# Linear attention and mixture of experts in one Trainium2 kernel: LayerNorm rows turned by a transposing DMA, k rows likewise, a new order within a step, own spare rows

## The chip, the cores and the metric

The kernel runs on one NeuronCore of a Trainium2 chip. The number that counts is the device time of one execution in microseconds (us); lower is better. TensorE is called PE below (its weight loads PEld), VectorE DVE, ScalarE ACT, GpSimd POOL and SyncE SP. SP computes nothing here: it issues DMAs, in order.

## The reference, cut to what matters

Shapes: x is 4 x 2048 x 256 in fp32. Attention has 16 heads of 16 features and is causal and linear; the feed-forward part has 8 experts with 512 hidden features, and each token goes to its best two.

```python
x = x + attn(layernorm(x))
    # q, k = elu(xWq + bq) + 1, elu(xWk + bk) + 1 ; v = xWv + bv
    # per token: s += k v^T ; z += k ; value = q s / (q z + 1e-6) ; out = value Wo + bo
x = x + moe(layernorm(x))
    # logits = x router^T ; top 2, softmax over them
    # out = sum over the two experts e of p_e * (gelu(x w1[e]^T + b1[e]) w2[e]^T + b2[e])
```

## The kernel before, in words

The kernel has two parts.

**Attention part** (about the first 640 us). The sequence is cut into 16 steps of 128 positions; a step holds the 4 batches, so 4 x 128 tokens. The work is software-pipelined over steps. In body c, the *front* handles step c (LayerNorm rows turned, q, k, v projections, feature map), the *back* handles step c-1 (scores within the chunk, attention, running state), `ro` finishes step c-2 (output projection, residual, second LayerNorm, router), and `sc` gives slots to the rows of step c-3 and scatters them to the experts' rows in DRAM. The first bodies are written out: body 0, then body 1 with the front alone, then body 1 with the back alone, then 2 to 4. Bodies 5 to 14 are a hardware loop with two bodies per round, and the rest is written out again.

The order on each engine is the order in which `body` writes it, one function per engine; semaphores join them. Nothing is rescheduled.

Values that need more than fp16 are split in two fp16 parts, high and low, and multiplied in three passes (`split3`). The names that matter:
- `xs`: x of one step as loaded; `xn`: its LayerNorm, with tokens on partitions (ACT, `normalise`, L748). PE turns `xn` (`x_transposes`, L442) into the banks pF, ACT takes the high part (`x_hi`, L787) and DVE the low part (`x_lo`, L1029) into `xT`, with features on partitions. `project(0..3)` (L422) reads `xT`.
- `feature(m)` (POOL, L1385) ends the feature map of q (m = 0, 1) and k (m = 2, 3); `qk_high` and `low` (L811, L1389) split it into `qkhl`. SP stores q, waits for the landing, loads the stack `qst` in 6 DMAs, then does the same for k with 3 DMAs into `kst` (L347, L363, L358). The scores (L494, L497) read both stacks.
- k with tokens on partitions: PE turns the fp32 `kf` (`k_rows`, L480) and ACT copies it to `kn` (L773). The state update reads `kn` and `v` in fp32 (L527).
- Scores: ACT takes the high part (`score_hi`, L781) and DVE the low part (`score_lo`, L1024), 16 of each a step. The second LayerNorm is applied on DVE (`norm2_apply`, L1037); the router's gap and second probability are two small DVE operations (L1108, L1125).

**Expert part** (from about 670 us). 71 tiles of 256 rows run in a loop. Each tile is loaded, turned, sent through two layers, and its rows are added to the output by indirect DMAs from POOL (L1485). Rows that fill up a tile, and whole tiles that fill up the 71, add zeros to one shared block of 256 spare output rows. POOL waits before a tile until as many earlier additions have landed as `settled` says (L1306): for a tile of an expert, those of all tiles ahead of that expert's first; for a tile behind the last expert, those of all tiles ahead of itself.

Of the kernel before, what the change touches and what calls it, by code (L numbers as in the profile page):

```python
# [50 lines left out]
C_POW, C_LN, C_PAD, C_TOKEN, C_END = 280, 284, 285, 287, 287 + STEPS * B  # L51
# [4 lines left out]
def constants():  # L56
# [11 lines left out]
    f[:, C_PAD:C_PAD + 2] = T + p[:, None] + P * np.arange(2)  # L68
# [11 lines left out]
def build(nc, x, wqkvo, bqk, bv, bo, rw, w1, b1, w2, b2, cf, ch, cb, out):  # L80
# [5 lines left out]
    with ExitStack() as ctx:  # L86
# [18 lines left out]
        pads = sb("pads", [P, 2, ROW], F32)  # L105

# [6 lines left out]
        v = sb("v", [P, 2, B, H, VC], F32, att)  # L113
# [21 lines left out]
        xn = sb("xn", [P, B, D], F32, att)  # L135
        xT = sb("xT", [P, 2, KC, B * C], F16, att)
        et = sb("et", [P, 2, B * C], F32, att)
        lt = sb("lt", [P, 2, B * C], F32, att)
        kn = sb("kn", [P, B, D], F32, att)
# [27 lines left out]
        spare = xn[:].rearrange("p b d -> p (b d)")  # L167
# [34 lines left out]
        route_copy = lambda c, b: xn[:, b] if c == STEPS + 1 else xn2T[:, b % 2].rearrange("p k n -> p (k n)")  # L202
# [7 lines left out]
        passed = {nc.vector.engine: sem("passed_dve"), nc.gpsimd.engine: sem("passed_pool")}  # L210
# [8 lines left out]
        pads_set, pads_out = sem("pads_set"), sem("pads_out")  # L219
# [5 lines left out]
        xT_ps, xT_hi, xT_lo = sem("xT_ps"), sem("xT_hi"), sem("xT_lo")  # L225
# [4 lines left out]
        kn_ps, kn_done = sem("kn_ps"), sem("kn_done")  # L230
# [12 lines left out]
        TAB = 19  # L243
# [69 lines left out]
        def _(sp):  # L313
# [9 lines left out]

            def body(j, c, front=True, back=True):
                i, _ = front_of(j, c)
                r, _ = front_of(j, c - 2)
                fr, ro, nx = front and real(j, c), real(j, c - 2), front and real(j, c + 1)
                for n in range(0 if c == 1 else 2 if c == 0 else 1 if nx else 0):

                    sp.wait_ge(xn_done, 4 * (i + n) + 4)  # L330
                    sp.dma_start(xs[:], x_steps[bass.ds(i + n + 1, 1)].rearrange("i p b d -> p (i b) d")).then_inc(x_in, 16)
# [3 lines left out]
                if fr:  # L335
# [5 lines left out]
                    for t, sent in enumerate((q_out, k_out)):  # L341
                        sp.wait_ge(qk_hi, 4 * i + 2 * t + 2)
                        sp.wait_ge(qk_lo, 4 * i + 2 * t + 2)
                        if c >= 2 and t == 0:

                            sp.wait_ge(stack_in[par], 144 * (j + c // 2))
                        sp.dma_start(qk_dram[par, t].rearrange("m p n -> p m n"), qkhl[:, t]).then_inc(sent, 16)  # L347
                        sp.wait_ge(sent, 16 * i + 16)
                        if t == 0 and c >= 2:
# [65 lines left out]
        def _(pe):  # L415
            def split3(out, lhs, rhs, n, parts=((0, 0), (0, 1), (1, 0)), low_wait=None):

                terms = [(a, b_, k) for a, b_ in parts for k in range(n)]
                for t, (a, b_, k) in enumerate(terms):
                    if low_wait and t == 2 * n:  # L420
                        pe.wait_ge(*low_wait)
# [3 lines left out]
            def body(j, c, front=True, back=True):  # L425
# [157 lines left out]
                if bk:  # L583
                    scores(0, 0)
# [941 lines left out]
```

## Time and profile before

| | |
|---|---|
| median of 3 runs | 1098.19 us (1097.6 to 1102.02) |
| profiled execution | 1098.38 us, span 1096.6 us |
| mean granted TensorE clock | 0.957 |
| busy: PE, DVE, ACT, POOL | 953.8, 823.6, 662.1, 695.6 us |
| DMA | 138.18 MB, mean 126 GB/s |

Busy time counts each engine's own instructions. In the profile an idle time is put down to what ended it, and a DVE or POOL instruction that has started but is held still counts as busy. The attention part and the expert part have different limits, so the shares of the whole span say little about either.

### The profile page before, as it was taken

Reading aid. Unit: us, or ns where it says so; the run is one execution under the profiler, and the core shown is the slowest. Engines: PE = TensorE matmul, PEld = TensorE weight load, DVE = VectorE, ACT = ScalarE, POOL = GpSimd, SP = SyncE. Lnnn points to the kernel's source line nnn. Section 1 sums busy time; section 2 is a strip of 40 time slices with the busy share of each in tenths; the row PEclk is TensorE's granted clock in tenths of the full one; section 3 lists DMA queues with packets and bytes.
Section 4 is the critical chain, followed back from the end, with each engine's and each line's share of the span. In section 5 each row is a group of like instructions: output and inputs, shape, how many; then the busy total and the mean of one; then the engine's idle time right before and its main releaser. Section 6 shows DMA issues by size and latency. Waiting matters only on the chain. (4 is left out here: it accounts for less than half of the span.)

```text
span 1096.6 us, 33544 instructions
## 1 busy us (share of the span) xinstructions
PE 953.8 (87%) x10092; PEld 786.4 (72%) x10093; DVE 823.6 (75%) x2201; ACT 662.1 (60%) x1253; POOL 695.6 (63%) x606
## 2 busy tenths in 40 slices
PE   4499888988897998889998935999999999999993
PEld 2277667766775775766677724999999999999992
DVE  5378999997997997988998874666666666666662
ACT  5567776776676676766775433555555555555550
POOL 5626576787677777775878452555665565665554
PEclk9989999999999998999999966999999999999997
DMA  3665766556654673664466282455555555555553
GB/s 110 151 139 129 201 166 155 130 154 170 151 124 134 161 162 112 169 159 111 148 143 163 72 320 77 87 96 96 89 91 94 92 96 96 87 92 95 92 87 38
DMA packets 124885, 138.18 MB, mean 126 GB/s; under 512 B 10320, under 2 KB 117968, under 8 KB 124176
## 3 DMA queue, kind: packets, MB, share of 16 engines
q1 hardware_dynamic: 96944, 100.26, 37.3%
q0 software_dynamic: 26688, 35.93, 17.7%
q10 hardware_dynamic: 1184, 1.18, 0.4%
q8 instruction: 29, 0.48, 0.2%
q14 instruction: 40, 0.33, 0.1%
HBM read 72.00 MB, written 65.34 MB: 125 GB/s over the span
## 5 line engine op out<-in xcount | busy, mean ns | idle before, releaser
L1485 POOL DMA_INDIRECT out<-yt,to_token x142 | 226.8, 1597 | 177.4 <-DVE yt L1349 108.7
L1024 DVE SCALAR_TENSOR_TENSOR ahl<-pS,ahl 128x512 f16<-128x512 f32 x240 | 161.4, 682 | 34.8 <-ACT ahl L781 33.1
L781 ACT ACTIVATE ahl<-pS 128x512 f16<-128x512 f32 x240 | 140.8, 599 | 71.1 <-PE pS L497 69.0
L1403 POOL DMA_INDIRECT expert_in<-xn,cur x128 | 130.7, 1021 | 35.2 <-issue 33.1
L422 PE MATMUL pF<-xT,was 128*128 128x512 f16 x384 | 104.6, 415 | 14.5 <-DVE xT L1029 14.4
L949 ACT ACTIVATE g<-pS,b1s 128x256 f32<-128x256 f32 x144 | 60.4, 471 | 90.6 <-PE pS L422 90.6
L494 PE MATMUL pS<-cbs 128*128 128x512 bf16 x240 | 94.4, 393 | 20.0 <-DMA kst<-qk_parts 14.2
L1320 DVE TENSOR_TENSOR ghl<-g,ghl 128x1024 f16<-128x1024 f32 x71 | 87.2, 1228 | 24.4 <-ACT ghl L971 24.4
L422 PE MATMUL pU<-w2s,ghl 128*128 x864 | 100.5, 273 | 1.9 <-DVE ghl L1320 1.9
L422 PE MATMUL pS<-gT,w1s 128*128 128x256 f16 x864 | 101.3, 274 | 0.1
L422 PE MATMUL pF<-w2s,ghl 128*128 x840 | 97.4, 273 | 0.0
L497 PE MATMUL pS<-qst,kst 96*128 96x256 f16 x480 | 94.8, 279 | 0.0
L422 PEld LDWEIGHTS pU<-w2s,ghl 128*128 128x128 f16 x864 | 84.4, 98 | 12.1 <-issue 2.5
L422 PEld LDWEIGHTS pS<-gT,w1s 128*128 x864 | 85.0, 98 | 10.8 <-issue 0.5
L1361 POOL TENSOR_TENSOR rs<-ve,cfs 128x4 f32<-128x4 f32 x32 | 33.0, 1031 | 93.1 <-DVE ve L994 93.1
L518 PE MATMUL pO<-vhl,ahl 128*128 128x17 f16 x3072 | 87.4, 171 | 2.1 <-DVE ahl L1024 2.1
L518 PEld LDWEIGHTS pO<-vhl,ahl 128*128 128x128 f16 x3072 | 85.6, 96 | 4.6 <-DVE ahl L1024 2.7
L422 PEld LDWEIGHTS pF<-w2s,ghl 128*128 128x128 f16 x840 | 82.2, 98 | 9.1
L422 PEld LDWEIGHTS pF<-xT,was 128*128 128x128 f16 x384 | 38.6, 104 | 55.3 <-issue 21.8
L971 ACT ACTIVATE ghl<-g 128x1024 f16<-128x1024 f32 x71 | 75.6, 1065 | 0.1
L497 PEld LDWEIGHTS pS<-qst,kst 96*128 96x128 f16 x480 | 48.5, 101 | 36.8 <-issue 5.2
L949 ACT ACTIVATE g<-pO,b1s 128x256 f32<-128x256 f32 x70 | 29.4, 470 | 71.6 <-PE pO L422 71.6
(160 smaller groups left out, 2308.8 us busy)
## 6 DMA issues: line engine op xcount, KB each, us to landing
xg<-expert_in SPq DMA_DIRECT2D x71, 260.0 KB, 3.0
qk_parts<-qkhl SPq DMA_DIRECT2D x32, 512.0 KB, 2.9
qst<-qk_parts SPq DMA_DIRECT2D x96, 128.0 KB
kst<-qk_parts SPq DMA_DIRECT2D x48, 256.0 KB
xs<-x SPq DMA_DIRECT2D x16, 512.0 KB, 5.1
xr<-x SPq DMA_DIRECT2D x16, 512.0 KB, 4.7
out<-x SPq DMA_DIRECT2D x16, 512.0 KB, 3.2
expert_in<-pads SPq DMA_DIRECT2D x16, 260.0 KB, 4.0
```

Of the source, the lines that this page charges most:

```text
L422: mm = nc.tensor.matmul(out, lhs(a, k), rhs(b_, k), start=(t == 0), stop=(t == len(terms) - 1))
L494: nc.tensor.matmul(o[:], ident16, mask16, start=True, stop=False, skip_group_check=True)
L497: mm = nc.tensor.matmul(o[:, e * 2 * C:(e + 1) * 2 * C], kst[0:STACK, sp_, pr, b * C:(b + 1) * C], qst[0:STACK, sp_, pr, :, b * C:(b + 1) ...
L518: mm = nc.tensor.matmul(pO[:, h * VC:(h + 1) * VC], ahl[:, b % 2, a, h * C:(h + 1) * C], vhl[:, sp_, b_, b, h * VC:(h + 1) * VC], start=False,
L781: nc.scalar.activation(ahl[:, b % 2, 0, n * 4 * C:(n + 1) * 4 * C], score_bank(fr, n)[:], ACT.Relu).then_inc(sc_hi, 1)
L949: nc.scalar.activation(g[:, p1, f], hidden[p1][f // 2][:, (f % 2) * MT:(f % 2 + 1) * MT], ACT.Gelu, bias=b1s[:, bass.ds(e * FC + f, 1)], s ...
L971: nc.scalar.activation(ghl[:, p1, 0].rearrange("p f n -> p (f n)"), g[:, p1].rearrange("p f n -> p (f n)"), ACT.Copy).then_inc(g_hi, 1)
L1024: V.scalar_tensor_tensor(ahl[:, b % 2, 1, cols], score_bank(fr, n)[:], 0.0, ahl[:, b % 2, 0, cols], ALU.max, ALU.subtract).then_inc(sc_lo, 1)
L1320: V.tensor_tensor(ghl[:, p1, 1].rearrange("p f n -> p (f n)"), g[:, p1].rearrange("p f n -> p (f n)"), ghl[:, p1, 0].rearrange("p f n -> p ...
L1361: G.tensor_tensor(rs[:], ve[:], cfs[:, C_POW:C_POW + B], ALU.pow).then_inc(done, 1)
L1403: G.indirect_dma_start(xg_dram, bass.IndirectOffsetOnAxis(ap=cur[:, qp, 2 * b + t:2 * b + t + 1], axis=0), xn2[:, qp, b], None).then_inc(s ...
L1485: G.indirect_dma_start(out, bass.IndirectOffsetOnAxis(ap=to_token[:, c % 2, s:s + 1], axis=0), yt[:, c % 2, s], None, compute_op=ALU.add). ...
```

## The change

1. **x.** ACT normalises `xs` in place and takes the high part of all four batches in one operation (`x_high`); DVE takes the low part in one operation (`x_low`) into `xhl`, still with tokens on partitions. SP issues one transposing DMA per step from `xhl` to `xT`, which is now double-buffered. All of this is done in the body before the one that uses it. PE's `x_transposes`, ACT's `x_hi` and DVE's `x_lo` are gone.
2. **k.** `kn` holds fp16 high and low parts and is filled by a transposing DMA from what SP stored of k in DRAM. PE's `k_rows` and ACT's copies are gone. The state update is three fp16 passes over `kn` and `vhl`, where it was one fp32 product.
3. **Order within a step.** The projections stand earlier on PE, the feature operations earlier on ACT, the statistics of the next step's x earlier on DVE, and both reciprocal roots in POOL stand in the middle.
4. **Spare rows.** The output has a block of 256 spare rows for each of the 8 possible filling tiles besides the shared one; the blocks are zeroed by 8 more DMAs of 256 KB in body 2, and one DMA in body 3 writes 2048 row numbers. `settled` is zero for filling tiles.
5. **VectorE forms.** `norm2_apply` was a TENSOR_SCALAR and two small router operations were TENSOR_TENSOR; all three are now SCALAR_TENSOR_TENSOR.
6. `v` has one buffer instead of two.

```diff
+            sp.wait_ge(x_lo, 1)
+            sp.dma_start_transpose(xT[:, 0]..., xhl[:]...).then_inc(xT_in, 16)
...
-                for n in range(0 if c == 1 else 2 if c == 0 else 1 if nx else 0):
-                    sp.wait_ge(xn_done, 4 * (i + n) + 4)
-                    sp.dma_start(xs[:], x_steps[bass.ds(i + n + 1, 1)]...).then_inc(x_in, 16)
+                if nx:
+                    sp.dma_start(xs[:], x_steps[bass.ds(i + 1, 1)]...).then_inc(x_in, 16)
+                if bk:
+                    if c >= 2:
+                        sp.wait_ge(u_ps, 4 * s)
+                    sp.dma_start_transpose(kn[:], qk_dram[(c - 1) % 2, 1]...).then_inc(kn_in, 16)
...     (q and k stored, stacks loaded, as before)
+                if turn_next:
+                    if c >= 1:
+                        sp.wait_ge(v_ps, 2 * i)
+                    sp.wait_ge(x_lo, i + 2)
+                    sp.dma_start_transpose(xT[:, (c + 1) % 2]..., xhl[:]...).then_inc(xT_in, 16)
...
+                        sp.dma_start(out[T + (n + 1) * MT:T + (n + 2) * MT]..., pads[:, :, 0:D]).then_inc(spare_out, 16)
...
                 def project(m):
                     if m == 0:
-                        pe.wait_ge(xT_lo, 2 * i + 1)
-                        pe.wait_ge(xT_hi, 2 * i + 2)
+                        pe.wait_ge(xT_in, 16 * i + 16)
...
-                    pe.wait_ge(kn_done, 2 * s + 2)
+                    if b == 0:
+                        pe.wait_ge(kn_in, 16 * s + 16)
...
-                        mm = nc.tensor.matmul(pU[...], kn[:, b, k * P:(k + 1) * P], v[:, sp_, b, ...], start=True, stop=True)
+                        mm = split3(pU[...], lambda a, _: kn[:, b, (KC * a + k) * P:...],
+                                    lambda a, _: vhl[:, sp_, a, b, ...], 1)
...
+            def x_high(i, first=False):
+                act.wait_ge(xn_done, 4 * i + 4)
+                if not first:
+                    act.wait_ge(xT_in, 16 * i)
+                nc.scalar.activation(xhl[:, :, 0], xs[:], ACT.Copy).then_inc(x_hi, 1)
...
+            def x_low(i):
+                dve.wait_ge(x_hi, i + 1)
+                V.scalar_tensor_tensor(xhl[:, :, 1], xs[:], 1.0, xhl[:, :, 0], ALU.mult, ALU.subtract).then_inc(x_lo, 1)
...
-                    V.tensor_scalar(xn2[:, rp, b, 0:D], x1[:, b], mv2[:, b, 0:1], rs2[:, b:b + 1], ALU.subtract, ALU.mult)
+                    V.scalar_tensor_tensor(xn2[:, rp, b, 0:D], x1[:, b], mv2[:, b, 0:1],
+                                           rs2[:, b:b + 1].to_broadcast([P, D]), ALU.subtract, ALU.mult)
...
-                    V.tensor_tensor(pd[:, 0], mx[:, :, 1], mx[:, :, 0], ALU.subtract)
+                    V.scalar_tensor_tensor(pd[:, 0], mx[:, :, 1], 1.0, mx[:, :, 0], ALU.mult, ALU.subtract)
...
-            chain(V.scalar_tensor_tensor(tj[0:1, 3], tj[0:1, 0], float(E), tj[0:1, 2], ALU.is_ge, ALU.mult))
-            chain(V.tensor_tensor(first_i[:, 0], tj[0:1, 1], tj[0:1, 3], ALU.add))
+            chain(V.scalar_tensor_tensor(first_i[:, 0], tj[0:1, 0], float(E), tj[0:1, 1], ALU.is_lt, ALU.mult))
```

`turn_next` is true in the bodies that prepare the next step: body 0, the second half of body 1, and every later body that has a next step.

The order on PE at the start of body 2 before (`pF<-cfs,xn` are the turns of x, `pU<-cfs,kf` those of k, `pF<-xT,was` a projection, `pS<-...` the scores, `pO<-...` the attention, `pU<-v,kn` the state update):

```order
L480 MATMUL pU<-cfs,kf 128x128 x4
L422 MATMUL pF<-xT,was 128x512 x6
L494 MATMUL pS<-cbs 128x512
L497 MATMUL pS<-qst,kst 128x256 x2
L422 MATMUL pA<-was,aT 128x256 x6
L422 MATMUL pF<-xT,was 128x512 x6
L494 MATMUL pS<-cbs 128x512
L497 MATMUL pS<-qst,kst 128x256 x2
L480 MATMUL pU<-cfs,kf 128x128 x4
```

The same place now, from the first projection's end on:

```order
L457 MATMUL pF<-xT,was 128x512 x6
L548 MATMUL pA<-cfs,at 128x128 x2
L505 MATMUL pS<-cbs 128x512
L508 MATMUL pS<-qst,kst 128x256 x2
L457 MATMUL pF<-xT,was 128x512 x6
L457 MATMUL pA<-was,aT 128x256 x6
L505 MATMUL pS<-cbs 128x512
L508 MATMUL pS<-qst,kst 128x256 x2
```

The turns of k have left PE, and the third projection stands right behind the third score group.

The order of SP's DMAs in bodies 0 and 1 before, from the load of the k stack of step 0:

```order
L358 DMA kst<-qk_parts 32x8x512 x3
L367 DMA w1raw<-w 128x512
L338 DMA xr<-x 128x4x256
L347 DMA qk_parts<-qkhl 128x4x512
L363 DMA qst<-qk_parts 16x8x512 x6
L347 DMA qk_parts<-qkhl 128x4x512
L358 DMA kst<-qk_parts 32x8x512 x3
```

The same stretch now:

```order
L378 DMA kst<-qk_parts 32x8x512 x3
L391 DMA_TRANSPOSE xT<-xhl 128x16x128
L396 DMA w1raw<-w 128x512
L339 DMA xs<-x 128x4x256
L352 DMA xr<-x 128x4x256
L366 DMA qk_parts<-qkhl 128x4x512
L383 DMA qst<-qk_parts 16x8x512 x6
L366 DMA qk_parts<-qkhl 128x4x512
L378 DMA kst<-qk_parts 32x8x512 x3
L345 DMA_TRANSPOSE kn<-qk_parts 128x4x512
```

The transposing DMA of step 1's x stands behind the first k stack, and that of step 0's k rows stands behind the second, whose data are step 1's.

## Rows read from the trace of the kernel before

**Rows 1.** Windows view, 13 steps, last line: total us, busy sums, then means per step.

```profile
sum 488.00, PE 437.06 PEld 338.80 DVE 436.79 ACT 349.70 POOL 348.16; mean PE 33.62 PEld 26.06 DVE 33.60 ACT 26.90 POOL 26.78
```

**Rows 2.** DVE groups by form, 100 to 560 us: busy, mean ns | idle before.

```profile
L1037 DVE TENSOR_SCALAR xn<-x,mv,rs 128x256 f32<-128x256 f32 x48 | 36.6, 803 | 0.0
L1108 DVE TENSOR_TENSOR pd<-mx 128x4 f32<-128x4 f32 x12 | 22.0, 1837 | 0.0
...
L1125 DVE TENSOR_TENSOR xn<-pd,one_exp 128x4 f32<-128x4 f32 x12 | 16.0, 1330 | 0.0
```

**Rows 3.** Tile xn: count, duration ns min/median/max, first and last start.

```profile
L1037 DVE TENSOR_SCALAR xn<-x,mv,rs x64: 398/410/1469, 91.0 to 639.0; 128x256 f32<-128x256 f32 x64
...
L1125 DVE TENSOR_TENSOR xn<-pd,one_exp x16: 155/1172/2177, 120.1 to 646.4; 128x4 f32<-128x4 f32 x16
```

**Rows 4.** POOL and DVE timelines at 257 us: start, us, operation [idle before <-releaser].

```profile
257.08 2.37 POOL L1365 TENSOR_TENSOR xr<-xr,bos 128x1024 f32<-128x1024 f32 x1
```

```profile
257.66 1.82 DVE L1108 TENSOR_TENSOR pd<-mx 128x4 f32<-128x4 f32 x1
...
263.75 1.29 DVE L1029 TENSOR_TENSOR xT<-pF,xT 128x512 f16<-128x512 f32 x2 [2.47 <-issue]
```

**Rows 5.** POOL and DVE timelines at 96 us.

```profile
96.43 2.72 POOL L1389 TENSOR_TENSOR qkhl<-kf,qkhl 128x512 f16<-128x512 f32 x2
```

```profile
96.49 1.65 DVE L1144 SCALAR_TENSOR_TENSOR w1s<-w1raw,w1s 128x512 f16<-128x512 f32 x1
```

**Rows 6.** PE timeline across the turn of the loop.

```profile
251.95 0.71 PE L527 MATMUL pU<-v,kn 128*128 128x136 f32 x4
...
253.42 1.47 PE L422 MATMUL pF<-was,xT 128*128 128x256 f16 x12
...
257.88 1.04 PE L442 MATMUL pF<-cfs,xn 128*128 128x128 f32 x8
...
261.69 0.60 PE L480 MATMUL pU<-cfs,kf 128*128 128x128 f32 x4
...
264.57 1.68 PE L422 MATMUL pF<-xT,was 128*128 128x512 f16 x5 [2.09 <-DVE xT L1029]
```

**Rows 7.** SP timeline, one step of the loop: issue times.

```profile
279.45 0.37 SPq L347 DMA_DIRECT2D qk_parts<-qkhl  x1
282.48 2.70 SPq L363 DMA_DIRECT2D qst<-qk_parts  x6
285.28 0.38 SPq L347 DMA_DIRECT2D qk_parts<-qkhl  x1
291.71 1.35 SPq L358 DMA_DIRECT2D kst<-qk_parts  x3
```

**Rows 8.** PE, POOL and SP timelines, bodies 0 and 1.

```profile
36.12 4.45 PE L422 MATMUL pF<-xT,was 128*128 128x512 f16 x12 [3.06 <-DVE xT L1029]
...
60.80 0.71 PE L527 MATMUL pU<-v,kn 128*128 128x136 f32 x4
```

```profile
46.56 1.16 POOL L1389 TENSOR_TENSOR qkhl<-qf,qkhl 128x512 f16<-128x512 f32 x1
```

```profile
48.48 1.29 SPq L358 DMA_DIRECT2D kst<-qk_parts  x3
...
60.67 0.38 SPq L347 DMA_DIRECT2D qk_parts<-qkhl  x1
67.20 1.30 SPq L358 DMA_DIRECT2D kst<-qk_parts  x3
```

**Rows 9.** Page, DMA issues: KB each, median us to landing.

```profile
expert_in<-pads SPq DMA_DIRECT2D x16, 260.0 KB, 4.0
```

**Rows 10.** POOL and DVE timelines, the last tiles.

```profile
1074.49 2.49 POOL L1485 DMA_INDIRECT out<-yt,to_token  x1 [2.65 <-DMA out<-yt,to_token]
...
1081.82 1.55 POOL L1485 DMA_INDIRECT out<-yt,to_token  x1 [2.79 <-DMA out<-yt,to_token]
...
1088.26 1.55 POOL L1485 DMA_INDIRECT out<-yt,to_token  x1 [2.83 <-DMA out<-yt,to_token]
```

```profile
1081.21 0.69 DVE L1344 SCALAR_TENSOR_TENSOR yt<-pU,b2s 128x512 f32<-128x512 f32 x1 [4.38 <-DMA out<-yt,to_token]
```

More of the change, by code:

```diff
@@ L373, in body @@
                                      pads[:]).then_inc(pads_out, 16)
+                        sp.dma_start(out[T + (n + 1) * MT:T + (n + 2) * MT].rearrange("(s p) d -> p s d", p=P),
+                                     pads[:, :, 0:D]).then_inc(spare_out, 16)
+                if c == 3:
+                    sp.wait_ge(pads_out, 16 * E)
+                    with nc.allow_non_contiguous_dma("one number per row"):
+                        sp.dma_start(xg_dram[DUMMY:ROWS, TOKEN:TOKEN + 1].rearrange("(s p) d -> p (s d)", p=P),
+                                     dummy_token[:]).then_inc(pads_out, 16)
                 if c == STEPS:
@@ L856, in body @@
                     w2_high(1)
+                if bk:
+                    score_hi(0, 2)
                 if fr and c >= 2:
@@ L907, in body @@
                     row_copy(3)
+                if turn_next:
+                    x_high(i + 1)
                 if bk:
                     score_hi(2, 3)
-                if bk:
                     score_hi(3, 0)
                     score_hi(3, 1)
-                left = c == 1 and not front
-                if nx and c != 1 or left:
-                    normalise(i + 1, 0)
-                if bk:
                     score_hi(3, 2)
@@ L920, in body @@
                     out_hi(s, 2)
-                if nx and c != 1 or left:
-                    normalise(i + 1, 1)
-                if fr and c != 1 or left:
+                if fr and c != 1 or c == 1 and not front:
                     v_high()
@@ L1018, in body @@
                 nx = front and real(j, c + 1)
+                turn_next = nx and c != 1 or c == 1 and not front
                 par, sp_, rp, qp = c % 2, (c - 1) % 2, c % 2, (c - 3) % 2
@@ L1414, in body @@
                     feature(0)
+                    feature(1)
+                    low(0)
                 if ro:
                     rstd(r, ve2, rs2, ln2_ve, ln2_rs)
+                if nx and c >= 2 or c == 1 and not front:
+                    rstd(i + 1, ve1, rs1, ln1_ve, ln1_rs)
                 if fr:
-                    feature(1)
-                    low(0)
                     feature(2)
```

250 lines of the change are left out of this document (110 added, 140 removed).

## The prediction

> **What bounds the kernel now.** I read the page's busy shares first, then a table of windows over the attention part, then DVE's groups, then timelines of single engines around each place that the change touches. The reader is to see two things. In the attention part PE and DVE are both nearly full: over 13 steps of 37.54 us (488.0 / 13) PE is busy 33.62 us and DVE 33.60 us a step [rows 1], so each is idle for 3.9 us. In the expert part PE alone is full and nothing there is changed but its last tiles. So the steps are won only as far as DVE gets shorter or idles less; relieving PE alone is not enough.
>
> Part of DVE's busy time is no work. The four-element operation L1125 takes 0.155 us at best and 1.33 us on average, L1037 0.40 at best and 0.80 on average [rows 2, 3]. L1108, of the same size as L1125, averages 1.84 us. One instance shows why: it starts at 257.66 and ends at 259.48, and the POOL operation that started at 257.08 ends at 259.45 [rows 4]. DVE is held until POOL is done. Per step that is 1.68 (L1108) + 1.18 (L1125) + 4 x 0.40 (L1037) = 4.5 us.
>
> **The change, part by part.** The sum is made against the profiled execution, 1098.38 us, 0.2 us above the median of the three runs.
>
> *PE's work.* The turns of x (1.04 us) and of k (2 x 0.60) go [rows 6]. A state update was 0.71 us for a pair in fp32. It becomes 6 fp16 matmuls of 136 columns; the row of 256 columns gives 0.12 us each (1.47 / 12), so at most 0.7 and by width 0.4 us: 4 x 0.3 = 1.2 saved, at least nothing. PE loses 2.2 to 3.4 us of work a step. On a DVE-bound step this counts only through DVE's idle time.
>
> *DVE's work.* Both `x_lo` go, 1.29 us [rows 4]. `x_low` has 1024 elements, as many as the two together, so 1.2 us. The statistics, moments and shift of the next step's x only move. Net: -0.1 us a step.
>
> *The VectorE forms.* Between none and all of the 4.5 us could go. The rows say none: L1144 already is a SCALAR_TENSOR_TENSOR with two SBUF inputs, and it took 1.65 us while a POOL operation begun 0.06 us ahead of it ran [rows 5], as a TENSOR_TENSOR does. All three new forms read two SBUF tensors. I take 0 for the form itself. What the new order does to these meetings I can't work out; POOL's work per step stays the same, and `x_low` is one more operation with two SBUF inputs, that can meet POOL's 2.37 us operation [rows 4]. I take 0, bounds 2.4 lost and 2.5 gained a step.
>
> By the Trainium skill (SBUF — State Buffer, "SBUF: two separate sides") the port pair that DVE shares with GpSimd is an exclusive lock, taken by a DVE operation in a two-port mode or with two SBUF inputs, the latter only against a GpSimd operation that reads SBUF. By that rule the new forms are held as the old ones were, which the trace's 1.65 us bears out; if the form decided, the steps would gain up to 4.5 us more.
>
> *DVE's idle time.* Of 3.9 us a step, at the turn of the loop 2.47 us stand ahead of `x_lo`, put down to "issue", every second step [rows 4], and PE waits 2.09 us for its result [rows 6]. Now PE has a score group and the first two projections to run without DVE there, since `xT` came a step earlier, so the restart behind the gap is quick, though DVE's own gap stays. The other idle is DVE waiting for scores, which PE reaches sooner by 2 to 3 us of freed work. I take 3.9 down to 2.1, so 1.8 gained a step; bounds 0 and 3.
>
> *ACT.* It loses two copies for x and two for k, and gains `x_high`. It was 26.90 us busy of 37.5 [rows 1]; hidden either way.
>
> *SP's queue in the loop.* Before, q's store was issued at 279.45, its stack at 282.48, k's store at 285.28, k's stack at 291.71 [rows 7]. k's store alone took 6.4 us, since it stood behind the q stack. By the new order on PE, where the third projection stands behind the third score group, I estimate the projections 8 us and, since POOL's features follow only in part, k's store 4 us earlier, which pays for the transposing DMA of x behind the k stack. That must land before the next step's first projection. By these rows I place its issue 8 us after k's store, and its landing 4 to 7 us later (512 KB; the like store took 3.0 us alone and 6.4 us in the queue). That is just at the start of the next step. I take no wait; the other end is a rival. The k rows' DMA is issued at the start of the body and needed behind four score groups and three projections, which I estimate at 12 us in.
>
> *The start.* This is the largest single term, and it is a loss. SP works in order, and the transposing DMA of step 1's x stands behind step 0's k stack. That was issued from 48.48 to 49.77 [rows 8]; I leave it there, within 3 us. With 4 to 5 us for landing, `project(0)` of step 1 starts at 54 where it started at 36.12. From that projection to the end of q's low parts it took 11.6 us (36.12 to 47.72), so q's store goes at 65.6, its landing takes 3, its stack 2.8 to issue, and k's store and stack follow 6.5 us apart (60.67 to 67.20): k's stack of step 1 at 78. The k rows of step 0 are asked for behind it, at 79, and land at 84. PE's first state update began at 60.80 and waits for them. That is 23 us. Even if nothing of step 1 came later, it would be 67.20 + 1.3 + 4.5 = 73, 12 us late; at slow transposes 28. PE is in order, and everything behind it in body 1 waits. I take +23.
>
> *Spare rows.* 8 more DMAs of 256 KB in body 2, and 2048 single numbers in body 3. DMAs of 260 KB land in 4.0 us each [rows 9]; 8 more at the rate of this size hold the rings some 7 us, in which the k rows of step 2 wait. There are about 12 us of slack. I take +2, bounds 0 and 6.
>
> *The last tiles.* POOL's idle time in front of three filling tiles' first additions, 2.65 + 2.79 + 2.83 us [rows 10], is a wait for the landing of the tile ahead. With own rows it goes. Next is DVE: it waited 4.38 us for the landing two tiles back (1081.21), which now comes earlier too. Not all is won, as POOL's additions then stand back to back behind the tile ahead: -6.5, bounds -5.5 and -8.3.
>
> Sum: 1098.4 + 23 + 2 - 6.5 - 14 x 1.8 (25.2; the 13 steps of the table and the next) = 1091.7, say **1092**.
>
> **The rivals.**
>
> *B. POOL's holds become rare.* The reorder or the new forms avoid most of the 4.5 us. For it: this is the only large time on DVE that is no work. Against it: L1144's row. Then 4.0 a step: 1098.4 + 18.5 - 56 = 1061.
>
> *C. The steps gain almost nothing (slower).* DVE stays as full as it is, because `x_low` is held behind POOL and PE's freed time turns into waits for DVE. For it: 33.60 busy of 37.54, and only 0.1 us of DVE's work goes. It decides when the gain per step is below 18.5 / 14 = 1.3 us, since the start must be paid for. With 0.5 a step: 1098.4 + 18.5 - 7 = 1110.
>
> *D. The transposing DMA lands late in every step.* PE's first projection then waits for it, and all behind it. The place has no slack by my reckoning, so each us beyond 7 costs 1 us a step. At 11 us from issue to landing a step gets 1.8 - 4 = 2.2 us longer and the start 31 us: 1098.4 + 31 - 4.5 + 31 = 1156. The trace of before has no such DMA; 512 KB in 3.0 us speaks against it, the 6.4 us in the queue for it. The Trainium skill gives both sides: VectorE: DVE Perf Modes, "The three transpose paths", has 1309 ns for one 128x128 block, so 21 us as an estimate for 16 blocks one after another; DMA: Bandwidth & Descriptors, "Latency and other measured facts", has 261 GB/s, an estimate of 2 us. No run here shows either yet.
>
> *E. The start costs less.* If body 1's front is not delayed, it is +12 instead of +23: 1081.
>
> **How the numbers follow.** Half a per cent is 5.5 us, about what a measurement of this kernel can tell from no change. Chances: forecast 0.34 (own range 1080 to 1104), B 0.18, C 0.28, D 0.12, E 0.08. Faster by over 0.5%: half of the forecast, B and E, 0.43. Within 0.5%: a third of the forecast and a quarter of C, 0.19. Slower: the rest of the forecast, of C, and D, 0.38. The range, 1064 to 1128, leaves out the far half of B and most of D.
>
> **What would show it.** Start: PE's first `pU` matmul waits for `kn` until 80 to 88. Steps: a mean of 35 to 36.5 us, DVE busy 33 to 34, with the new L1099 (the gap) and L1116 still far above 0.16 us when POOL computes; under B they fall to it. Under D the first projection of each step waits for DMA `xT`. Tail: POOL's last additions no longer wait for a landing, and 5.5 to 8 us go. The forecast is wrong if PE doesn't wait at the start, or if a step comes out under 34.5 or over 37 us.

## The result and the profile after

The changed kernel takes 1203.47 us (median of 4 runs, 1202.7 to 1208.27), the kernel before 1097.89 us beside it (1095.53 to 1102.02). The ratio is 1.098, 95% interval 1.0945 to 1.1017. I had forecast 1092, with a range up to 1128. Ratios leave out disturbed runs; so for two kernels below (`fixed` and `thin_old`) the ratio is lower than the median alone would give.

| | before | after |
|---|---|---|
| span of the profiled execution | 1096.6 us | 1206.5 us |
| mean granted TensorE clock | 0.957 | 0.904 |
| busy: PE, DVE, ACT, POOL | 953.8, 823.6, 662.1, 695.6 | 964.2, 824.2, 636.3, 698.1 us |
| step 4, DVE's first reciprocal of the attention | 200.1 us | 250.7 us |
| step 14, the same | 577.4 us | 687.0 us |

No engine got more work to speak of. The time is idle time, 110 us of it ahead of 690 us: 51 in the first five bodies, 59 in the ten steps of the loop. The last steps lose 6 more (the first addition of the expert part is issued at 802.8 us, before at 687.1), and the last tiles win 6 back. The last row of the windows view, 12 steps from 166.7 us on, answers to [rows 1]: total, busy sums, means per step.

```profile
sum 520.30, PE 408.97 PEld 294.87 DVE 405.47 ACT 300.74 POOL 335.62; mean PE 34.08 PEld 24.57 DVE 33.79 ACT 25.06 POOL 27.97
```

A step takes 43.36 us (520.3 / 12) where it took 37.54. PE and DVE are busy about as before; each is idle for 9.3 us and more where it was 3.9. So neither bounds the step: they wait for each other. PE's own figure hides a change: the turns of x and k are gone and the state update is shorter, 2.7 us less a step together, but the rest of its matmuls, the same in number, took 3.2 us more. The granted clock was 0.86 to 0.96 in these steps, where it was 0.92 to 1.00.

DVE's groups by form, 100 to 700 us (busy, mean ns | idle), and beneath them the durations (min/median/max ns) by tile. They answer to [rows 2, 3].

```profile
L1027 DVE SCALAR_TENSOR_TENSOR xn<-x,mv,rs 128x256 f32<-128x256 f32 x56 | 33.9, 645 | 0.0
L1003 DVE SCALAR_TENSOR_TENSOR xhl<-xs,xhl 128x1024 f16<-128x1024 f32 x13 | 31.4, 2418 | 0.0
L1099 DVE SCALAR_TENSOR_TENSOR pd<-mx 128x4 f32<-128x4 f32 x13 | 24.0, 1850 | 0.0
...
L1116 DVE SCALAR_TENSOR_TENSOR xn<-pd,one_exp 128x4 f32<-128x4 f32 x13 | 7.4, 566 | 0.0
```

```profile
L1027 DVE SCALAR_TENSOR_TENSOR xn<-x,mv,rs x64: 471/480/1174, 119.9 to 754.5; 128x256 f32<-128x256 f32 x64
...
L1003 DVE SCALAR_TENSOR_TENSOR xhl<-xs,xhl x16: 1214/2924/3071, 13.5 to 662.8; 128x1024 f16<-128x1024 f32 x16
```

The new form is held behind POOL like the old one (L1099, 1.85 us on average), and the low part of x, 1.21 us at best, takes 2.9 in about half of the steps. One meeting of L1099 with POOL, in the two timelines, answers to [rows 4, 5]:

```profile
319.46 2.24 POOL L1395 TENSOR_TENSOR vhl<-v,vhl 128x1088 f16<-128x1088 f32 x1 [0.96 <-PE pO L529]
```

```profile
319.93 1.80 DVE L1099 SCALAR_TENSOR_TENSOR pd<-mx 128x4 f32<-128x4 f32 x1
```

Where PE stands still in the loop, PE timeline (answers to [rows 6]):

```profile
295.57 0.39 PE L505 MATMUL pS<-cbs 128*128 128x512 bf16 x1 [0.76 <-DVE ahl L1018]
...
298.62 0.39 PE L505 MATMUL pS<-cbs 128*128 128x512 bf16 x1 [1.02 <-DVE ahl L1018]
...
313.54 0.61 PE L505 MATMUL pS<-cbs 128*128 128x512 bf16 x1 [2.18 <-DVE ahl L1018]
...
324.16 0.61 PE L505 MATMUL pS<-cbs 128*128 128x512 bf16 x1 [3.75 <-issue]
```

Two things: a score group waits for DVE's low part of the group two before (both use one bank), and at the turn of the loop, ahead of 324.16, PE waits for nothing that a semaphore shows. The waits view, 225 to 650 us, sums the first (engine, line <- what ended the wait: us, times, longest); beneath it the same of before, 225 to 610 us.

```profile
ACT ahl L785 <- PE pS L508: 137.2, 56, 7.4
DVE ahl L1018 <- ACT ahl L785: 62.8, 53, 4.6
...
PE pS L505 <- DVE ahl L1018: 50.4, 50, 2.2
```

```profile
ACT ahl L781 <- PE pS L497: 41.1, 58, 5.3
...
DVE ahl L1024 <- ACT ahl L781: 19.3, 39, 3.3
...
PE pS L494 <- DVE ahl L1024: 4.3, 4, 1.1
```

Both stretches hold some ten steps. PE, ACT and DVE hand the scores round in a ring: 4.3 us of PE's waits there have become 50.4. No line in that stretch has PE wait for `xT` or `kn`.

The start, SP and PE timelines, answers to [rows 8]:

```profile
44.36 1.30 SPq L378 DMA_DIRECT2D kst<-qk_parts  x3
45.78 3.53 SPq L391 DMA_TRANSPOSE xT<-xhl  x1
...
76.61 1.30 SPq L378 DMA_DIRECT2D kst<-qk_parts  x3
77.96 3.91 SPq L345 DMA_TRANSPOSE kn<-qk_parts  x1
96.96 1.94 SPq L391 DMA_TRANSPOSE xT<-xhl  x1
```

```profile
51.49 8.28 PE L457 MATMUL pF<-xT,was 128*128 128x512 f16 x24 [18.68 <-DMA xT<-xhl]
...
83.98 0.86 PE L457 MATMUL pU<-vhl,kn 128*128 128x136 f16 x6 [12.85 <-DMA kn<-qk_parts]
```

SP in one step of the loop, which began at 250.7, answers to [rows 7]:

```profile
264.91 1.34 SPq L378 DMA_DIRECT2D kst<-qk_parts  x3
270.65 3.51 SPq L391 DMA_TRANSPOSE xT<-xhl  x1
...
277.46 3.98 SPq L345 DMA_TRANSPOSE kn<-qk_parts  x1
```

The k stack is asked for 14 us into the step (16 before), and `xT` only 6 us behind it, as `x_low` is done no sooner; it is there in time.

In body 3, DVE and PE timelines:

```profile
158.73 1.41 DVE L992 BATCH_NORM_STATS2 st<-xs 128x6 f32<-128x256 f32 x4 [9.57 <-DMA xs<-x]
```

```profile
160.94 1.44 PE L457 MATMUL pA<-was,aT 128*128 128x256 f16 x6 [10.42 <-DVE x L1067]
```

x's load was issued at 153.02, behind 16 zeroing DMAs (140.29 to 152.98). Before, it was issued at 114.78 and also stood right behind the zeroing, which was 8 DMAs (108.73 to 114.73); but its statistics stood late on DVE. So the change made the queue ahead of the load twice as long, and moved the load's reader forward. The 4.0 us of [rows 9] is a median over 16 issues, half of them from a later place: those in body 2 landed in 4.8 to 6.4 us, and the 8 new ones land in 4.0 to 4.8.

The tail, POOL timeline, answers to [rows 10]:

```profile
1189.34 1.55 POOL L1473 DMA_INDIRECT out<-yt,to_token  x1 [1.77 <-DMA out<-yt,to_token]
...
1193.81 1.55 POOL L1473 DMA_INDIRECT out<-yt,to_token  x1 [0.88 <-DMA out<-yt,to_token]
...
1198.29 1.55 POOL L1473 DMA_INDIRECT out<-yt,to_token  x1 [0.88 <-DMA out<-yt,to_token]
```

The three waits of 2.65 to 2.83 us are down to 1.77, 0.88 and 0.88.

### The profile page after: what moved, and what is told of

Same layout as the page of the kernel before. It is cut to its first block, busy times and chain, and to the rows that moved or that the text cites. A ratio compares the mean times of both kernels' runs of the same rounds, so it can differ in the third digit from the quotient of the medians.

```text
span 1206.5 us, 33214 instructions
## 1 busy us (share of the span) xinstructions
PE 964.2 (80%) x9964; PEld 766.3 (64%) x9965; DVE 824.2 (68%) x2184; ACT 636.3 (53%) x1205; POOL 698.1 (58%) x606
## 3 DMA queue, kind: packets, MB, share of 16 engines
q10 hardware_dynamic: 1184, 1.18, 0.3%
## 4 chain that ended last, share of the span: by engine, by line
PE 57%; DVE 16%; issue 10%; ACT 7%; DMA 5%; SPq 2%; POOL 1%; ACTq 0%; POOLq 0%; DVEq 0%
PE pF L457 15%; PE pU L457 9%; PE pS L457 7%; PE pO L529 5%; PE pA L457 5%; DVE ahl L1018 4%; PE pO L457 4%; DVE xhl L1003 3%; PE pS L505 3%; ACT ahl L785 2%; PE pS L508 2%; DVE xn L1027 2%; DMA qk_parts<-qkhl 2%; PE pR L573 1%; ACT et L793 1%
## 5 line engine op out<-in xcount | busy, mean ns | idle before, releaser
L505 PE MATMUL pS<-cbs 128*128 128x512 bf16 x240 | 100.8, 420 | 85.2 <-DVE ahl L1018 66.9
L1390 POOL DMA_INDIRECT expert_in<-xn,cur x128 | 142.7, 1115 | 34.8 <-issue 31.0
L1383 POOL TENSOR_TENSOR state<-state,ut 128x272 f32<-128x272 f32 x64 | 48.6, 759 | 94.6 <-DVE ut L1050 94.3
L508 PE MATMUL pS<-qst,kst 96*128 96x256 f16 x480 | 100.8, 294 | 0.0
L505 PEld LDWEIGHTS pS<-cbs 128*128 128x128 bf16 x240 | 25.0, 104 | 108.3 <-DVE ahl L1018 83.7
L1372 POOL TENSOR_TENSOR qf<-et,lt 128x512 f32<-128x512 f32 x32 | 40.6, 1269 | 74.7 <-ACT et L799 74.3
L457 PE MATMUL pA<-was,aT 128*128 128x256 f16 x384 | 55.4, 283 | 28.7 <-DVE x L1067 24.0
```

What stands on the lines that cost most here:

```text
L457: mm = nc.tensor.matmul(out, lhs(a, k), rhs(b_, k), start=(t == 0), stop=(t == len(terms) - 1))
L505: nc.tensor.matmul(o[:], ident16, mask16, start=True, stop=False, skip_group_check=True)
L508: mm = nc.tensor.matmul(o[:, e * 2 * C:(e + 1) * 2 * C], kst[0:STACK, sp_, pr, b * C:(b + 1) * C], qst[0:STACK, sp_, pr, :, b * C:(b + 1) ...
L1372: G.tensor_tensor(feature_rows(m, par), et[:, m % 2], lt[:, m % 2], ALU.add).then_inc(qk_f, 1)
L1383: G.tensor_tensor(sb_, sb_, ut[:, b % 2], ALU.add).then_inc(state_new, 1)
L1390: G.indirect_dma_start(xg_dram, bass.IndirectOffsetOnAxis(ap=cur[:, qp, 2 * b + t:2 * b + t + 1], axis=0), xn2[:, qp, b], None).then_inc(s ...
```

## The experiments

Each was timed beside the kernel before. A hundredth of the ratio is 11 us.

| kernel | median us | ratio to before, 95% interval |
|---|---|---|
| changed kernel | 1203.5 | 1.098, 1.0945 to 1.1017 |
| code_after | 1197.5 | 1.094, 1.091 to 1.0969 |
| order_old | 1187.1 | 1.0838, 1.08 to 1.0877 |
| small_dma | 1191.6 | 1.0863, 1.0828 to 1.0897 |
| start_order | 1174.7 | 1.0715, 1.068 to 1.075 |
| xs_first | 1189.5 | 1.0851, 1.082 to 1.0882 |
| thin_old | 1168.9 | 1.0623, 1.0551 to 1.0695 |
| thin_all | 1163.3 | 1.0597, 1.0522 to 1.0672 |
| split_x | 1177.0 | 1.0729, 1.0671 to 1.0787 |
| late_x | 1220.8 | 1.1139, 1.1087 to 1.1192 |
| fixed | 1147.2 | 1.0375, 1.0301 to 1.0449 |
| mid_x | 1135.5 | 1.0375, 1.0321 to 1.0429 |
| after_unrolled | 1180.1 | 1.0743, 1.0703 to 1.0783 |
| mid_unrolled | 1129.0 | 1.0268, 1.0197 to 1.0339 |
| k_by_dma | 1116.9 | 1.0182, 1.0146 to 1.0217 |
| code_before | 1115.5 | 1.0173, 1.0153 to 1.0194 |
| forms_before | 1100.1 | 1.0030, 1.0004 to 1.0057 |
| spare_before | 1088.9 | 0.9930, 0.9905 to 0.9955 |
| unrolled | 1086.2 | 0.9893, 0.9856 to 0.993 |

### PE's code: code_after, code_before

```diff
             pe.wait_ge(consts_in, CONSTS)
+            for _ in range(230):          # 115 instructions; 256, so 128, in code_before
+                pe.wait_ge(cf_in, 16)
             iterations(pe, body)
```

> The changed kernel, with 115 instructions that only wait (for something long there) put in PE's program ahead of its first body, where PE is idle until about 40 us anyway. Nothing else differs. In the changed kernel's profile PE stands still for 3.75 us at a turn of the attention loop with no releaser ('issue'), and queue q8 of kind 'instruction' brings nine packets of 16 KB in every round of the loop, where before it brought none between 253 and 569 us. Theory L (the loop's code no longer lies in PE's buffer as a whole, because it now starts at another place against the 16 KB pieces in which it is fetched): moved by 115 instructions it covers one piece less, the fetches in the loop go, the gaps at the 4 turns go with them, 4 x 3.75 = 15 us and up to 25 us with what the other engines lose behind them: 1178 to 1190 us. Rival N (the gap is due to a late semaphore that the profile does not show, as the order of the work has changed): 1203 us, fetches as they are.

> The kernel before, with 128 such waiting instructions at the same place. Theory L: its loop of code now covers one 16 KB piece more and no longer fits, so nine or so fetches a round appear and PE waits about 3.7 us at each of the 4 turns: 1110 to 1122 us against 1098. Rival N: 1098 us, no fetches in the loop.

DMA queue rows of kind "instruction" (packets, MB, share), 260 to 560 us: of before, of the changed kernel, of code_before, and of code_after (320 to 600 us).

```profile
q14 instruction: 19, 0.16, 0.2%
```

```profile
q8 instruction: 29, 0.48, 0.8%
q14 instruction: 19, 0.16, 0.2%
```

```profile
q8 instruction: 35, 0.57, 0.8%
q14 instruction: 20, 0.16, 0.2%
```

```profile
q14 instruction: 17, 0.14, 0.2%
```

The fetches follow the place of the code: they go in one kernel and appear in the other, and with them PE's gap at the turn. PE timeline of code_before, at a turn:

```profile
354.02 1.96 PE L442 MATMUL pF<-cfs,xn 128*128 128x128 f32 x8 [4.86 <-issue]
```

So the cause of PE's gap is shown, but its price was not as expected. code_after's median fell by 6.0 us, and the intervals of the two ratios overlap; the 13.5 us between the two profiled spans compare the slowest of four executions with the fastest of four. With PE's gap gone another shows at the turn, DVE's. DVE timelines of before, code_after and k_by_dma at a turn:

```profile
339.63 1.29 DVE L1029 TENSOR_TENSOR xT<-pF,xT 128x512 f16<-128x512 f32 x2 [2.82 <-issue]
```

```profile
321.33 1.29 DVE L1020 SCALAR_TENSOR_TENSOR ahl<-pS,ahl 128x512 f16<-128x512 f32 x2 [3.00 <-issue]
```

```profile
359.89 1.29 DVE L1017 TENSOR_TENSOR xT<-pF,xT 128x512 f16<-128x512 f32 x2 [5.08 <-issue]
```

In code_before most of the 18.4 us are not the turns: PE's first matmul starts at 21.7 us instead of 12.75, with nothing that it waits for, since the 128 waiting instructions themselves take time where PE is needed early (in code_after they had room: 20.3 us, and 20.4 without them). Its ten steps grew by 4.4 us only (381.7 against 377.3), as PE's gap lies beside DVE's.

The Trainium skill (Runtime: NRT & Kernel Launch, "Instruction fetch mechanics") has 16 KiB blocks of 256 instructions and a buffer of 128 KiB for PE, 32 KiB for most others, and says that a taken branch to a target outside the current window of two blocks forces a fetch. The 16 KB packets of q8 agree. The window does not fit PE: its loop of 1706 instructions in the kernel before jumps back over more than two blocks, and q8 brought nothing; the measurement decides. Which engine q14 serves is not shown. Its packets are of 8 KB; in the kernel before three of them start from 261.7 to 266.9 us, where DVE's gap [rows 4] lasts from 261.3 to 263.75, and so at each turn.

### The turns away: after_unrolled, unrolled

```diff
-            for c in range(2, LOOP0):
-                body(0, c)
-            with engine.Fori(0, (LOOP1 - LOOP0) // 2) as j:
-                for c in (LOOP0, LOOP0 + 1):
-                    body(j, c)
-            for c in range(LOOP1, END):
+            for c in range(2, END):
                 body(0, c)
```

> The changed kernel (1203.5 us) with the attention part's loop written out; nothing else. At its 4 turns PE has a gap of 3.75, 4.01, 5.02 and 5.46 us with no releaser, 18.2 us in all, and DVE waits beside it. Theory T and L (both are code fetched at a jump): all of it goes, 16 to 22 us less, 1181 to 1187; moving PE's code by 115 instructions brought only 6.0 of the median, since DVE's own gap of 3.0 us then showed at each turn. Rival: 1195 to 1203.

> spare_before (1088.9 us) with the attention part's loop written out, all 16 steps one after another. At each of its 4 turns DVE stands still for 2.4 to 3.5 us with no releaser after its first small instruction, while packets of 8 KB of kind 'instruction' arrive on queue q14. Theory T (a jump back makes DVE fetch its code anew): written out, the four gaps go, and 3 of the 4 times 2.6 us reach the end: 8 to 10 us less, 1079 to 1081. Rival (straight code of this length streams no faster than it runs, and other fetches take their place): 1085 to 1092.

In the changed kernel the turns cost 23.4 us of the median, slightly more than forecast; its steps are then 40.7 and 41.2 us by turns, where 41.1 and 47.7 stood. Written out, PE's code still comes in 16 KB packets (29 from 230 to 620 us), but no gap of over 1 us without a releaser is left: what stops PE is the fetching behind a jump, not fetching as such. In the kernel before (with spare rows) 2.8 us of the median go, less than forecast and not clear of the scatter, as the intervals of the two ratios overlap. The ten steps of the two profiles do not show the gain either: 368.0 us with the loop, 375.2 without (in executions of 1085.9 and 1091.2 us).

### The start and the load of x: start_order, xs_first

```diff
-                if bk:                                    # kn(c-1)
+                if bk and c != 1 or c == 1 and front:     # start_order
...
                     for t, sent in enumerate((q_out, k_out)):
+                        if c == 0 and t == 1:
+                            sp.wait_ge(x_lo, 2)
+                            sp.dma_start_transpose(xT[:, 1]..., xhl[:]...)   # start_order
...
                 if c == 2:
+                    sp.dma_start(xs[:], x_steps[bass.ds(i + 2, 1)]...)        # xs_first
                     sp.wait_ge(pads_set, 3)
```

> code_after with two DMAs moved on SP: xT(1) ahead of the store of k(0) instead of behind the k stack of step 0 (x_lo(1) is there at 37.3, it is issued at 45.8), and kn(0) ahead of q's store of step 1 instead of behind its k stack (issued at 78). If the start term is right (PE's first state update at 84.0 where it was at 60.8): kn(0) lands by 52, that wait of 12.9 us goes, xT(1) lands 7 us earlier, 15 to 23 us less than code_after's 1197.5: 1175 to 1183. If what follows takes it back (xs(2) or the stacks are the next to be late): 1185 to 1193.

> code_after with x's load of body 3 issued at the end of body 2 ahead of the 16 DMAs that zero the spare and filling rows, not behind them. In the changed kernel those stand in SP's queue from 140.3 to 153.0, and DVE, whose statistics of the next x now come third in the body, waits 9.6 us for xs, PE 10.4. Theory: 8 to 10 us less than 1197.5: 1188 to 1190. Rival (the next transfers behind the zeroing, kn(2) at 153.9 and xr, hold PE as long): 1194 to 1198.

PE timeline of start_order:

```profile
45.81 8.13 PE L461 MATMUL pF<-xT,was 128*128 128x512 f16 x24 [12.38 <-DMA xT<-xhl]
65.31 0.84 PE L461 MATMUL pU<-vhl,kn 128*128 128x136 f16 x6
```

The first state update runs at 65.3 us and not at 84.0 (60.8 in the kernel before), and 22.8 us of the median go: most of the loss at the start was the place of two DMAs in one queue. Step 4's attention matmuls still start 30 us later than in the kernel before (228.7 against 198.5), as the bodies after it are longer too. xs_first gains 8.0, as expected.

### The transfers or the order: small_dma, order_old

```diff
-                    sp.dma_start_transpose(kn[:], qk_dram...)
+                    sp.dma_start(kn[:, 0, 0:32], qk_dram[(c - 1) % 2, 1, 0, :, 0:32])   # in the loop's bodies; xT likewise
```

> code_after (the changed kernel with 115 waiting instructions ahead of PE's first body: 1197.5 us, pairs of steps in the loop 85.4 us), with both transposing DMAs of the loop's 10 bodies replaced by plain DMAs of 8 KB in the same place of SP's program; bodies 0 to 4 and those behind the loop as they are. Left out: x and k of the loop's steps are not turned, so xT and kn hold old values. Theory D (the turned transfers cost the time: 80 packets of under 512 B for every 10 others, DMA share 0.63 to 0.72 against 0.58, issue 2.5 to 2.9 us each on SP, everything behind them in SP's queue late): 2 to 4 us a step, 20 to 40 us less, 1160 to 1178. Theory O (PE's wait for the low parts of the scores, in a ring of two banks with less of PE's own work between): 1190 to 1198 us.

```diff
                 scores(0, 1)
-                project(1)
...
+                project(0)
                 scores(0, 2)
-                project(2)
                 out_project(r, 3)
+                project(1)
                 scores(0, 3)
                 scores(1, 0)
+                project(2)
                 attend(0)
```

> The changed kernel (with the 115 waiting instructions of code_after), with the projections on PE, the feature operations on ACT and POOL and the first low parts on DVE back in their old order; x and k are still turned by DMA, a step ahead, and the statistics stay early. Theory O (the new order makes PE wait for the low part of the scores: 0.76 + 1.02 + 0.39 + 0.76 + 2.18 us a step, of which the step before lost 1 to 2): 3 to 4 us less a step over 14 steps, 40 to 56 us below code_after. Rival M (the transposing DMAs cost the time, through SP's queue and the DMA load): within 10 us of code_after.

With both turned transfers of the loop away 6 us go (8 by the ratio): they are not what holds the steps. The old order gives 10.4 us, a quarter of what theory O claimed. Only a part of PE's wait for the low parts comes from the order, and another wait grows in its place, that for DVE's `at`. PE's waits from 225 to 650 us, of code_after, order_old and thin_old (next section but one):

```profile
PE pS L505 <- DVE ahl L1020: 41.0, 46, 2.3
```

```profile
PE pS L505 <- DVE ahl L1019: 26.2, 27, 1.9
PE pA L548 <- DVE at L1042: 22.0, 18, 2.5
```

```profile
PE pA L548 <- DVE at L1044: 20.0, 17, 2.4
PE pS L505 <- DVE ahl L1021: 16.7, 13, 2.2
```

In order_old `x_low` is seldom held (median 1.28 us, where it was 2.92 in the changed kernel), so its meetings with POOL came with the new order.

### k alone, forms alone, spare rows alone

> The kernel before, with part 2 of the change alone: k is turned by the transposing DMA, PE's and ACT's turns go, and the state update is three fp16 passes; order, x, spare rows and VectorE forms as before (20 waiting instructions keep PE's loop at its old place among its 16 KB pieces). In the first step kn(0) stands on SP behind the k stack of step 1, as in the changed kernel: 67.2 + 1.3 + about 3.9 + 5 = 77 against 60.8, +13 to +23 at the start. In the steps: theory D +1 to +3 us each, in all 1125 to 1160; theory O (k's turns were filler in the ring of the score banks, their going changes nothing): 0 in the steps, 1110 to 1120.

> The kernel before with part 5 of the change alone: norm2_apply and two router operations on DVE as SCALAR_TENSOR_TENSOR. My prediction gave the forms nothing, since a two-input form is held behind POOL like the others: 1097 us, within 3. If they avoid the hold (4.5 us of DVE a step): 1060 to 1085. If the longer least time of the form (0.47 against 0.40 us, four a step) shows: +3 to +5.

> The kernel before, with the spare rows alone: eight more blocks in the output, 8 zeroing DMAs in body 2, the row numbers in body 3, 'settled' zero for filling tiles. Its PE program is that of before. My prediction's terms: tail -5.5 to -8.3, the 8 DMAs +0 to +6: -6.5 + 2 = -4.5, so 1093.5 us. If the pads block the queue ahead of the load of x in the kernel before as they do in the changed one (there DVE waits 9.6 us for xs in body 3): about +3, 1101 us.

k_by_dma: its ten steps in the loop take 379.9 us against 377.3, so k's part costs the steps next to nothing; PE waits 13.14 us for the first `kn` (until 74.8), and that is most of the loss. The forms: 3.3 us slower, the interval just clear of 1, as the longer least time would have it. The spare rows: 7.7 us faster by the ratio. From the first addition of tile 60 (counted from 0) to the end it is 61.1 us instead of 67.0, so 5.9 of it is the tail; the rest is within the scatter. The zeroing alone, with x's reader at its old place, cost nothing that shows.

### Where x is prepared: thin_old, thin_all, split_x, late_x, mid_x

```diff
-                nc.scalar.activation(xhl[:, :, 0], xs[:], ...)         # x_high; x_low likewise
+                nc.scalar.activation(xhl[:, :, 0, cols], xs[:, :, cols], ...)   # thin_old: 8 columns in the loop's bodies
+                nc.scalar.activation(xhl[:, 2 * half:2 * half + 2, 0], xs[:, 2 * half:2 * half + 2], ...)   # split_x
```

> order_old (1187 us; 15 steps at 41 to 45 us for a body pair of 85), with the two new operations on x in the loop's 10 bodies made narrow: ACT takes the high part and DVE the low part of 8 columns in place of 256 (ACT 1.05 us, DVE 1.2 to 2.9 us a step go). Left out: the rest of x's split in those bodies, so their xT holds old values. Theory X (the split of x as one block of work in the middle of the step, between DVE's low parts of the scores, holds PE: 2.2 us wait for ahl, and lets the clock fall): 2 to 3 us a step, 20 to 30 us less, 1157 to 1167. Rival (it only fills DVE's idle time, 8 us a step): within 5 us of 1187.

> thin_old (1169 us, loop 402 us over its ten steps, before 377) with the statistics and normalise of x on 8 columns too in the loop's bodies. Left out: the rest of those operations there, so the loop's x values are not the LayerNorm's. Theory P (the early place of x's preparation costs what is left: 4 x 0.41 us of statistics stand ahead of the second LayerNorm's rows on DVE, for which PE waits 1.0 to 1.4 us a step, and ACT's 4 x 0.63 stand between the high parts): 1.5 to 2.5 us a step less, loop 377 to 387, 1144 to 1154. Rival K (what is left comes from the three-pass state update and the missing turns, which spread PE's work worse): within 5 us of 1169.

> order_old with the high and the low part of x in two halves each, of two batches: ACT's behind each pair of normalise, DVE's apart by two low parts of the scores. Theory X: the block that holds PE is halved, 0.5 to 1.5 us a step, 1170 to 1180. Rival: 1187.

> order_old with all preparation of the next x back at its late place: statistics behind the second attention on DVE, root on POOL behind the last feature, normalise on ACT around the last scores, high and low part at the body's end; so the transposing DMA of x is issued at the very end of a body. Theory P (what costs the steps 4 us is the early place of x's statistics, normalise and split among the scores): the wait of the projection for xT, some 4 to 8 us a step, replaces it; if P is right the steps lose less elsewhere, 39 to 42 us a step in all, 1150 to 1190. Rival L2 (the place does not matter, the DMA's 5 us then simply come on top): 46 us a step, 1230 to 1260.

> fixed, with x's preparation in the last half of the body in place of the first: statistics behind the second LayerNorm's rows, root on POOL behind the last feature, normalise and high part ahead of and between the last scores, the low part's halves around DVE's last low parts. Theory P: 1 to 2 us a step from the early place come back, while the transposing DMA now starts some 3 us ahead of the body's end and the first projection waits for it for 2 to 4 us a step: 1135 to 1165, that is, no clear gain on fixed. If the wait for xT decides as in late_x: 1165 to 1175.

Without the split's two operations, ACT 1.05 and DVE 1.2 to 2.9 us a step, order_old gets 18 to 24 us faster, about 2 us a step, and PE's wait for the low parts falls from 26.2 to 16.7 us: so the block lies on the ring. Halved and spread, it costs half. Statistics and normalise narrow as well give 3 to 5.5 us more, within what these kernels scatter. Theory P, as I put it, fails: it had 1.5 to 2.5 us a step for them.

late_x answers rival D's question, PE timeline:

```profile
340.51 2.74 PE L457 MATMUL pF<-xT,was 128*128 128x512 f16 x6 [6.37 <-DMA xT<-xhl]
```

Prepared late, as in the kernel before, the transfer does hold PE, for 5.7 to 6.4 us in each of the three steps from 290 to 390 us, and the kernel is 34 us slower than order_old. mid_x, in between, is no better than `fixed` by the ratio.

### The sum: fixed, mid_unrolled

> The changed kernel with all four remedies found: old order of the projections and features, x's split in halves (split_x: 1177 us), xT(1) and kn(0) earlier on SP (-22.8 alone), x's load of body 3 ahead of the zeroing (-8.0 alone), PE's loop of code moved. If the parts add up: 1177 - 22.8 - 8.0 = 1146 us. If two of them cured the same wait: 1150 to 1160.

> mid_x (1135.5 us) with the attention part's loop written out, so without the 115 waiting instructions. DVE's gaps at the 4 turns are 3.0 to 3.5 us there, 13 us in all: if they reach the end as in the kernel before (1088.9 to 1086.2, a quarter) 1131; if as in the changed kernel (1203.5 to 1180.1, with PE's gaps), up to 1122. Below 1120 would mean that the turns cost this kernel more than the gaps show.

`fixed` is old order, split_x, start_order and xs_first together. The parts add up within the scatter: from the ratios of the parts 1.0415, measured 1.0375 (1.0301 to 1.0449), some 1137 us. mid_unrolled ends at 1129.0, 2.7% above the kernel before, and that with the spare rows in it. So about 74 us of the loss are mended; 31 us are left against the kernel before, 43 against `unrolled`, which has the spare rows too. Of these 43 us, 12.5 lie in bodies 2 to 4 (127.2 us against 114.7 in `unrolled`) and 17 in the ten steps after (391.9 against 375.2). From 240 to 400 us PE waits there for DVE's `at` (8.6 us in 8) and for `xT` (7.0 in 3), and DVE 22.2 us for ACT's high parts; which move causes which was not tried, and the cause of this rest stays open. The fastest kernel of all is `unrolled`, the kernel before with the spare rows and no loop: 1.1% faster than before.

## Why the prediction was wrong

- **The start, +23: right** in size, place and kind. PE's first update came at 84.0, as worked out, and undoing the place brought it to 65.3 and gave 22.8 us back. One thing more hung on it: `xT(2)` was issued at 96.96 only, as `x_low` stood on DVE behind that update; PE did not wait for it.
- **The steps, -25: the step that failed.** I took the step as bound by DVE's and PE's work, let DVE's idle time fall from 3.9 to 2.1 us "because PE reaches the scores sooner", and bounded it by 0 and 3, with no room for a loss. It rose to 9.6 us, and a step took 5.8 us more. DVE's work was right to 0.3 us (33.79 where I had 33.5). PE's was not: I had 30.2 to 31.4 and it was 34.08; the work that I struck off did go (2.7 us), but the rest ran at a lower granted clock. Order was not in the sum at all. k's turns on PE lay between score groups, and taking them away won nothing in the steps (k_by_dma, 379.9 us for ten against 377.3); that the same holds for x's turns was not tried. The new blocks on ACT and DVE lie within the ring. I had priced `x_low` by its 1.2 us of work, not by who stands behind it: two score groups and an attention. Taken out of kernels that differ in other things, the parts measured are 23 us for the turns of the loop, 18 for the split of x and 10 for the order, of the 81 us that 14 steps of 5.8 make; about 30 stay open. With 23 for the start, 8 for the zeroing and 6 won at the tail the whole is 106 us, and 105.6 were measured.
- **DVE's holds, 0: right in sum, partly by luck.** They make 4.0 us a step, where it was 4.5. L1099 is held as before (1.70 us beyond its least time); L1027 loses 0.17 each instead of 0.40, and L1116 0.41 instead of 1.18; `x_low` came in their stead with 1.20. By the Trainium skill (SBUF — State Buffer, "SBUF: two separate sides") two SBUF inputs are enough for the hold, against a GpSimd operation that reads SBUF; L1099's 1.80 us at 319.93, beside such an operation, bears that out.
- **The forms, 0:** +3.3 by forms_before, hardly clear of nothing. The least time of the new form, 0.471 us against 0.398, would give 4.7 in 64 such operations; I had left it out.
- **Spare rows, +2, bounds 0 and 6:** mis-sized. I looked at what the zeroing delays among the transfers that existed, k's rows, and not at the load of x behind it on SP, whose reader the change had moved ahead on DVE: 8.0 us.
- **The tail, -6.5:** right; 67.0 to 61.1 us from tile 60 to the end.
- **The turn of the loop: "DVE's own gap stays"** was right, but I counted PE's restart as a gain. PE's loop, 1706 instructions before and 1663 now, starts about 100 instructions earlier, and so it was fetched anew in every round; the turns cost 23 us in all (after_unrolled), PE's and DVE's gaps together. I had no term for it, and did not ask why before's `q8` brought nothing in the loop.
- **Rivals.** D's mechanism (the first projection waits for `xT`) did not occur in the loop; late_x shows that it would have, without the early preparation, and the early preparation is the price paid to avoid it. The transfer landed in 5.3 us (median, `kn`; 4.3 to 7.7): of the two estimates from the Trainium skill the 261 GB/s of DMA: Bandwidth & Descriptors ("Latency and other measured facts", 2 us) is too low and the 1309 ns a block of VectorE: DVE Perf Modes ("The three transpose paths", 21 us in a row) far too high. C said that PE's freed time turns into waits for DVE, the right mechanism; it stopped at "nothing gained". None but D said that a step could get longer, and D for another reason. "Over 37 us a step" was named as the sign of a wrong forecast, and it was.

Also the clock, which I had left out of the sum: granted 0.904 against 0.957 over the whole span. In the rows of PE above, a matmul of 512 columns takes 0.39 us at 295.57, behind a wait of 0.76 us, at a granted clock of 1.00 (2.4 GHz); it takes 0.61 at 313.54, behind a wait of 2.18 us, at 0.50 (1.2 GHz). So PE has less to do than before and is busy as long.

## What to carry to other kernels

In a ring of engines with few banks, an operation costs what waits behind it, not its duration: list for each moved operation which hand-over it now stands in front of, and give every idle-time term a bound on the side of a loss. When work moves a step ahead, follow its inputs through every queue: both large losses in single bodies were one DMA behind others in SP's order, and moving a few lines mended most of them. When a loop gets slower with a gap at its turn that nobody releases, compare the instruction-fetch packets of the two profiles first.

## What I had not expected of the hardware

- A loop whose PE code was 1663 instructions long was fetched anew each round or not at all, depending on 115 instructions ahead of it. PE's gap at the turn was 3.75 to 5.46 us (changed kernel) and 4.1 to 4.9 us (code_before).
- DVE's gap at the same turn was 2.5 to 3.5 us before, 2.3 to 2.5 in small_dma, and 4.9 to 5.1 in k_by_dma, where a transposing DMA is issued 3.9 us ahead of the gap. That the transfer holds up the code is a guess; no run separates the two.
- The transposing DMA of 512 KB landed in 5.3 us (median) and took SP 1.3 to 4.9 us to issue, where a plain one of the same size took 0.4 (median).
